# Three-pass fp32r gate and up products in the shared experts of a two-layer perceiver kernel

## The chip, the cores and the metric

The kernel runs as one program on one core of a Trainium2 chip. The metric is the device time of that core in microseconds (us), from the start to the end of an execution; lower is better.

## The reference, cut to what matters

The program computes two layers, each a cross attention, a self attention and a feed-forward step on 512 rows of 512 features. The change touches the feed-forward step of the first layer, a mixture of experts: a router picks 8 of 64 experts for each row, and a shared expert, twice as wide, sees all rows. In short:

```python
scores = sigmoid(x @ gate_w.T)                      # x: 512 rows of the layer norm, E = 64
choice = scores + gate_bias
gmask  = the 4 of 8 groups with the largest sum of their two best choices
topk   = the 8 best of choice * gmask               # weights: scores, normed, times 2.5
routed = sum over e of rw[:, e] * (silu(x @ Wg[e].T) * (x @ Wu[e].T)) @ Wd[e].T   # I = 352
shared = (silu(x @ Sg.T) * (x @ Su.T)) @ Sd.T                                     # 704 wide
x = x + routed + shared
```

All inputs and outputs are fp32.

## The kernel before, in words

Each engine has its own instruction list, written out by hand, and waits on semaphores. Rows are held in four tiles of 128 (`NT = 4`), features in four chunks of 128 (`NC = 4`). `xnT` holds the normed rows turned, features on partitions.

The shared expert is split into two halves of width 352, and with four row tiles that makes eight pieces, k = 0 to 7, with tile t = k // 2 and half hf = k % 2. For each piece TensorE makes a gate group and an up group (`shared_in(k, 0)` and `shared_in(k, 1)`, matmuls at line 755), ScalarE takes the Silu of the gate (`shared_silu`, line 923), VectorE multiplies it with the up product (`shared_mul`, line 1044), TensorE turns the result (`shared_turned`, line 765), ScalarE copies it (`shared_ht`, lines 842 and 843), TensorE multiplies it with the down weights (`shared_out`, line 774) and VectorE adds it to `x` (`shared_add`, line 1048). Matmuls of plain fp32 data are issued twice each, so that a group over four chunks is eight matmuls in the profile.

The pieces are woven by hand into the routing. The routing runs on VectorE as one chain, lines 1055 to 1164, each operation waiting for the one before: scores, group choice, the best 8, the selection table `sel` (line 1091), the weights, then the ranks within the experts that TensorE counts with matrices of ones (lines 800 and 803), the slots, `eot` (line 1119: which expert each tile of rows belongs to), and four steps of one-hot operands (lines 1148 to 1154) from which TensorE makes the index and weight table (`table`, line 781). `shared_mul(0)` stands in this chain ahead of line 1071, `shared_mul(1)` ahead of line 1082, `shared_mul(2)` behind line 1091, `shared_mul(3)` and (4) around line 1122, `shared_mul(5)` behind the second of the four steps, (6) and (7) behind the tables. On TensorE pieces 0 to 5 stand ahead of or between the tables, 6 and 7 behind them.

GpSimd's list ends, in this stage, with the powers of the layer norm (line 337); then come two subtractions for the weights of the next layer (`rest`, line 1261, called with `wkv`), whose rounded halves ScalarE makes at line 932, and then the gathers of rows for the experts (line 2167).

SyncE's list: it writes the normed rows and a block of zeros to DRAM (lines 546 and 547, semaphore `rows_out`), then clears the accumulators (lines 548 and 550), then, when the tile table is known, starts the expert weights. `load_gu(0, 0)`, `load_dn(0, 0)` and `load_gu(0, 1)` wait for nothing more; `load_dn(0, 1)` (line 2118) waits for the last up group of the shared expert (`sh_u` = 8), since its buffer lies in `xnT`; what follows is queued behind it.

The expert loop already works in three passes of fp32r: an operand is rounded to fp32r by ScalarE ("high", `weights_high`, line 2078, `rows_high`, line 2300, `down_high`, line 2335), the rest is made by VectorE ("low", `weights_low`, line 2086, `rows_low`, line 2387), and TensorE adds high x high, high x low and low x high (line 2233). An fp32r matmul is issued once; a group over four chunks is twelve matmuls. At line 2078 the weights of the first expert are rounded into the buffer `wgu_hi[0]`, between `shared_ht(5)` and `shared_silu(6)`.

Of the kernel before, what the change touches and what calls it, by code (L numbers as in the profile page):

```python
# [26 lines left out]
P = 128  # L27
# [26 lines left out]
def perceiver(nc, a, out):  # L54
# [3 lines left out]
    with ExitStack() as ctx:  # L58
# [3 lines left out]
        def sem(name):  # L62
            return ctx.enter_context(nc.semaphore(name))
# [171 lines left out]
        wdn_hi = [m.view(2, D) for _ in range(2)]  # L235
        hT_lo = m.view(2, P)

        wkv_hi, wkv_lo = ([square(S_r, slot_at(i), NC) for i in ii] for ii in ((0, 2), (1, 3)))
# [41 lines left out]
        wbd_ready = sem("wbd_ready"); zpad_set = sem("zpad_set"); rix_ready = sem("rix_ready"); dve_x = sem("dve_x")  # L280
        dve_seq3 = sem("dve_seq3"); dve_seq4 = sem("dve_seq4"); pool_seq4 = sem("pool_seq4")
        ff_x = sem("ff_x"); ff_y = sem("ff_y")
        lg_made = sem("lg_made"); lg_exp = sem("lg_exp"); sel_ready = sem("sel_ready"); rank_made = sem("rank_made")
        ab_ready = sem("ab_ready"); tab_made = sem("tab_made"); eot_ready = sem("eot_ready")
        eot_made = sem("eot_made"); tables = sem("tables"); n_ready = sem("n_ready"); rows_out = sem("rows_out"); acc_out = sem("acc_out")
        sh_g = sem("sh_g"); sh_u = sem("sh_u"); sh_silu = sem("sh_silu"); sh_h = sem("sh_h")
        sh_t = sem("sh_t"); sh_ht = sem("sh_ht"); sh_d = sem("sh_d"); sh_y = sem("sh_y")
# [221 lines left out]


        def first_sync(sp):
            for c in range(NC):
# [39 lines left out]
        def first_pool(pool):  # L552
# [49 lines left out]
            for t in range(NT):  # L602
                ln_pow(pool, 2, t)

        def first_pe(pe):
# [144 lines left out]
            def shared_in(k, gu):  # L750
                t, hf = k // 2, k % 2
                if k >= 2:
                    pe.wait_ge(sh_h if gu else sh_silu, k - 1)
                for c in range(NC):
                    last = nc.tensor.matmul(PS[:, 2 + 2 * hf + gu, 0:I], xnT[:, c, t * P:(t + 1) * P],  # L755
                                            wgu[2 + hf][:, c, gu, :], start=(c == 0), stop=(c == NC - 1))
                last.then_inc(sh_u if gu else sh_g, 1)
# [87 lines left out]
        def first_act(act):  # L845
# [24 lines left out]
            def z_c(L, t):  # L870
                zt_copy(act, NT * L + t, t)

            rows_c(0, 0)
            rows_c(0, 1)
# [35 lines left out]
            z_c(1, 2)  # L910
            probs_c(1, 3)
            z_c(1, 3)
            for t in range(NT):
# [4 lines left out]
            def shared_silu(k):  # L918
# [4 lines left out]
                nc.scalar.activation(sgate[hf], PS[:, 2 + 2 * hf, 0:I], ACT.Silu).then_inc(sh_silu, 1)  # L923

            shared_silu(0)
            for k in range(1, 6):
                shared_silu(k)
                shared_ht(act, k - 1)
                if k == 2:
                    act.wait_ge(ld_wkv, 32)  # L930
                    for i in range(2):
                        nc.scalar.copy(wkv_hi[i], slot[1 + 2 * i][:, :, :]).then_inc(w_hi, 1)
            shared_ht(act, 5)
            weights_high(0, 0)
            shared_silu(6)
            shared_silu(7)
# [3 lines left out]
        def first_dve(dve):  # L940
# [222 lines left out]
            dve.wait_ge(tables, 1)  # L1163
            nc.vector.tensor_copy(cols[:, :, 1], idx_tab[:, 0:NBUF]).then_inc(cols_set, NBUF)  # L1164
            weights_low(0, 0)
            shared_mul(6)
            shared_mul(7)
# [921 lines left out]
        with nc.Block() as block:  # L2089
# [203 lines left out]
            def _(act):  # L2293
# [35 lines left out]
                def down_high(r, k):  # L2329

                    i = NBUF * r + k
                    act.wait_ge(w_dn[k], 32 * (r + 1))
                    if not (isinstance(r, int) and r == 0 and k < 2):
                        act.wait_ge(y_made, i - 1)
                    nc.scalar.copy(wdn_hi[k % 2], wdn[k][:, 0:2, :]).then_inc(dh_ready, 1)
# [175 lines left out]
```

## Time and profile before

| what | value |
|---|---|
| median of 3 runs | 1648.01 us (1646.71 to 1651.56) |
| the profiled execution | 1653.6 us, its span 1651.8 us |
| granted TensorE clock, mean | 0.993 of full speed |
| TensorE busy (matmul) | 1599.3 us, 97% |
| VectorE busy | 1096.3 us, 66% |
| ScalarE busy | 821.3 us, 50% |
| GpSimd busy | 465.2 us, 28% |
| HBM read and written | 207.81 MB and 21.76 MB |

The profile is of one execution, taken by the hardware profiler. Engines are PE (TensorE matmuls), PEld (TensorE weight loads, which overlap PE), DVE (VectorE), ACT (ScalarE), POOL (GpSimd) and SP (SyncE; SPq is its queue of transfers). Times in rows are microseconds from the start of the span unless a column says otherwise. L755 is line 755 of the kernel; S, R and PS are the large SBUF arenas and the PSUM tensor. Busy shares are means over the whole span: the stage of the change lies between about 117 and 210 us, and what a change in it is worth is read from that stage. Matmul ends are modelled, and the spans of GpSimd are rough.

### The profile page before, as it was taken

The numbers are of one execution on the slowest core, as the hardware profiler recorded it, in microseconds if no ns is written. First come the engines' busy times: TensorE is split into PE (matmuls) and PEld (weight loads), VectorE is DVE, ScalarE is ACT, GpSimd is POOL, SyncE is SP. The second block draws the span as 40 slices with busy tenths as digits, with TensorE's granted clock in tenths as the row PEclk, the third lists the DMA queues.
The fourth block names the chain that finished last, engine by engine and source line by source line (L and its number), as shares of the span: only waits on it lengthen the run. The fifth ranks groups of instructions, "written<-read, shape, count | busy, mean of one in ns | idle before, by whom it ended". The sixth has DMA issues, their size and how long they took to land.

```text
span 1651.8 us, 35385 instructions
## 1 busy us (share of the span) xinstructions
PE 1599.3 (97%) x13652; PEld 1406.2 (85%) x13653; DVE 1096.3 (66%) x2217; ACT 821.3 (50%) x1248; POOL 465.2 (28%) x421
## 2 busy tenths in 40 slices
PE   8999999999999999899999999999999999999897
PEld 5666688888888888769999999999999999999583
DVE  3878787787787788655656556565565655656666
ACT  1242177777777777324545445454354544634122
POOL 3012134444544544231413214132041320410100
PEclk9999999999999999999999999999999999999999
DMA  8003399999999999400202002020020100201200
GB/s 308 7 2 122 105 369 337 336 341 343 344 328 339 330 335 314 128 6 3 79 7 81 6 2 81 7 81 7 1 81 7 61 26 2 81 2 42 94 27 26
DMA packets 68858, 214.63 MB, mean 130 GB/s; under 512 B 13618, under 2 KB 31282, under 8 KB 58880
## 3 DMA queue, kind: packets, MB, share of 16 engines
q1 hardware_dynamic: 54400, 196.03, 34.1%
q0 software_dynamic: 14336, 16.83, 4.5%
q8 instruction: 93, 1.52, 0.4%
q14 instruction: 29, 0.24, 0.0%
HBM read 207.81 MB, written 21.76 MB: 139 GB/s over the span
## 4 chain that ended last, share of the span: by engine, by line
PE 81%; DMA 9%; DVE 5%; issue 2%; ACT 1%; SPq 1%; POOL 0%; ACTq 0%; DVEq 0%; POOLq 0%
PE PS L1352 17%; PE PS L1343 17%; PE PS L2233 10%; PE PS L1387 6%; PE PS L1368 6%; PE PS L2259 4%; PE PS L1410 3%; PE PS L400 3%; PE PS L2255 3%; PE PS L458 2%; DMA qbd<-in_w_gu 2%; DMA S<-in_w_gu 2%; DMA R<-in_w_gu 2%; PE PS L421 1%; PE PS L755 1%
## 5 line engine op out<-in xcount | busy, mean ns | idle before, releaser
L1352 PE MATMUL PS<-S_r 128*128 128x256 f32 x2496 | 319.4, 282 | 0.0
L1352 PEld LDWEIGHTS PS<-S_r 128*128 128x128 f32 x2496 | 309.7, 188 | 3.4 <-issue 0.5
L1343 PE MATMUL PS<-S_r 128*128 128x384 f32 (+1 forms) x1536 | 306.5, 349 | 0.0
L1539 DVE SCALAR_TENSOR_TENSOR kq<-PS,bias_c,kq 64x384 fp32r<-64x384 f32 (+1 forms) x256 | 162.3, 634 | 206.7 <-ACT kq L1470 201.9
L1343 PEld LDWEIGHTS PS<-S_r 128*128 128x128 f32 x1536 | 268.3, 188 | 6.5 <-issue 0.5
L2233 PE MATMUL PS<-S_r,R_r 128*128 128x352 f32 x1152 | 273.5, 328 | 0.2 <-DVE R_r L2387 0.2
L1470 ACT ACTIVATE kq<-PS,bias_c 64x384 fp32r<-64x384 f32 (+1 forms) x256 | 151.1, 590 | 197.1 <-PE PS L1343 193.7
L2233 PEld LDWEIGHTS PS<-S_r,R_r 128*128 128x128 f32 x1152 | 198.6, 188 | 3.8 <-DVE R_r L2387 0.5
L2180 POOL DMA_INDIRECT moe_acc<-x,cols x64 | 125.0, 1953 | 220.2 <-ACT x L2318 130.3
L1280 POOL COPY S<-qbd 64x128 f32<-64x128 f32 x128 | 38.3, 299 | 486.0 <-PE PS L1368 467.2
L1261 POOL TENSOR_TENSOR S_r<-S,S_r 128x1536 fp32r<-128x1536 f32 (+2 forms) x31 | 116.9, 3781 | 130.9 <-ACT S_r L1461 107.7
L1549 DVE CUSTOM_DVE_ANT_0 R<-PS,maskadd 128x384 f32<-128x384 f32 (+1 forms) x256 | 136.9, 572 | 3.6 <-PE PS L1368 0.4
L1490 ACT COPY S<-PS 128x512 f32<-128x512 f32 (+1 forms) x128 | 64.6, 505 | 129.0 <-PE PS L1387 127.2
L1484 ACT ACTIVATE R<-R,nmx 128x1601 f32<-128x1601 f32 x64 | 104.0, 1628 | 38.2 <-DVE nmx L1557 37.8
L1368 PE MATMUL PS<-kq 128*128 128x384 f32 (+1 forms) x512 | 120.3, 355 | 2.1 <-POOL kq L1285 1.3
L2086 DVE TENSOR_TENSOR R_r<-R,S_r 128x1408 fp32r<-128x1408 f32 x64 | 101.1, 1622 | 31.7 <-ACT S_r L2078 31.6
L1387 PE MATMUL PS<-ident,R 128*128 128x128 f32 (+1 forms) x832 | 114.9, 275 | 0.0
L2167 POOL DMA_INDIRECT S<-moe_rows,cols x64 | 95.7, 1495 | 68.3 <-DVE cols L1164 32.6
L2078 ACT CAST S_r<-R 128x1408 fp32r<-128x1408 f32 x64 | 84.5, 1368 | 45.9 <-DMA R<-in_w_gu 42.0
L1530 DVE COPY R<-PS 128x256 f32<-128x256 f32 (+1 forms) x124 | 52.5, 424 | 75.6 <-PE PS L1352 75.2
L1584 DVE COPY S<-PS 128x512 f32<-128x512 f32 (+1 forms) x128 | 75.2, 588 | 41.2 <-PE PS L1387 38.8
L1387 PEld LDWEIGHTS PS<-ident,R 128*128 128x128 f32 (+1 forms) x832 | 94.3, 140 | 7.3 <-DVE S L1584 2.2
(250 smaller groups left out, 2610.6 us busy)
## 6 DMA issues: line engine op xcount, KB each, us to landing
R<-in_w_gu SPq DMA_DIRECT2D x34, 1408.0 KB, 16.7
R<-in_w_dna SPq DMA_DIRECT2D x50, 512.0 KB, 17.2
qbd<-in_w_gu SPq DMA_DIRECT2D x16, 1408.0 KB
S<-in_w_gu SPq DMA_DIRECT2D x16, 1408.0 KB
S<-in_ctxT SPq DMA_DIRECT2D x24, 768.0 KB, 4.7
R<-in_w_dnb SPq DMA_DIRECT2D x50, 192.0 KB, 18.7
xnT<-in_w_dna SPq DMA_DIRECT2D x16, 512.0 KB
S<-in_ctxT SPq DMA_DIRECT2D x8, 898.0 KB
```

What stands on the lines that cost most here:

```text
L1261: nc.gpsimd.tensor_tensor(lo, raw, hi.bitcast(F32), ALU.subtract).then_inc(s, 1)
L1343: last = nc.tensor.matmul(PS[:, bank, 0:n], w3[0][:, cc, f0:f0 + P], x3[i][:, cc, 0:n], start=(cc == 0 and w3 is wkv_hi and x3 is ctx_hi), ...
L1352: last = nc.tensor.matmul(PS[:, bank, 0:256], x3[need][:, cc, k0:k0 + P], w3[1][:, cc, f0:f0 + 256], start=(cc == 0 and w3 is wkv_hi and x ...
L1368: last = nc.tensor.matmul(PS[:, p, 0:n], qb[(dc + 1) % 2][half][:, p, :], keys[c % 2][p][:, 0:n], start=(half == 0), stop=(half == 1))
L1387: last = nc.tensor.transpose(PS[0:n, 2 + p, i * P:(i + 1) * P], sx[2 * (dc % 2) + p][:, kt * P:kt * P + n], ident[:, :])
L1470: nc.scalar.activation(keys[c % 2][p][r, 0:n], PS[r, bank_of(b, dc, ("k", c)), 0:n], ACT.Identity, bias=bias_c[r, 3, f:f + 1]).then_inc(kh ...
L1484: nc.scalar.activation(v, v, ACT.Exp, scale=SC, bias=nmx[:, p:p + 1], accum_out=rsx[:, p:p + 1]).then_inc(px_ready, 1)
L1539: nc.vector.scalar_tensor_tensor(out=k[other, 0:n], in0=PS[r, bank_of(b, dc, ("k", c)), 0:n], scalar=bias_c[r, 3, f:f + 1], in1=k[r, 0:n]. ...
L1549: nc.vector.tensor_tensor_reduce(out=sx[2 * ((dc + 1) % 2) + p][:, k0:k0 + n], in0=PS[:, p, 0:n], in1=maskadd[:, k0:k0 + n], scale=1.0, sc ...
L2086: nc.vector.tensor_tensor(wgu_lo[k][:, c, :, :], wgu[k][:, c, :, :], wgu_hi[k % 2][:, c, :, :].bitcast(F32), ALU.subtract).then_inc(wl_rea ...
L2180: pool.indirect_dma_start(out=acc[k % 2], out_offset=bass.IndirectOffsetOnAxis(ap=cols[:, k, 0:1], axis=0), in_=yrow[k], in_offset=None, b ...
L2233: last = nc.tensor.matmul(PS[:, gu, 0:I], x3[:, c, :], w3[:, c, gu, :], start=(c == 0 and x3 is hi[0] and w3 is hi[1]), stop=(c == NC - 1 ...
```

## The change

Gate and up of pieces k = 2 to 7 are made from rounded and rest operands in three fp32r passes, as in the expert loop. Pieces 0 and 1 stay as they were.

- ScalarE rounds the weights of half 1 in one copy ahead of the last attention copy (`shared_high(1)`), and, behind a wait for the row writes (`rows_out` 32), the rows of tile 1 and the weights of half 0 ahead of `shared_silu(0)`, the rows of tiles 2 and 3 behind it. Rounded rows of tile 1 go where the normed rows lay, those of tiles 2 and 3 and the weights of half 1 into idle parts of `qbd` and `kq`, the weights of half 0 into `wgu_hi[0]`.
- GpSimd makes the rests in place, in the order of `SH_LO`: three of rows (512 elements a partition), four of weights (1408 elements), ahead of its two subtractions for `wkv`.
- TensorE waits for `sh_lo` before each of the twelve groups, and issues twelve matmuls in place of eight.
- Since `wgu_hi[0]` is in use until the up group of piece 6, `weights_high(0, 0)` moves behind `shared_silu(6)` and a wait for `sh_u` = 7, and `weights_low(0, 0)` behind `shared_mul(6)`. The first `down_high`, which writes into `kq`, waits for `sh_u` = 8.

```diff
@@ -234,6 +234,10 @@
         m = Arena(kq[:, :])
         wdn_hi = [m.view(2, D) for _ in range(2)]
         hT_lo = m.view(2, P)
+        sgu_hi = [wgu_hi[0], Arena(kq[:, :]).view(NC, 2, I)]
+        sgu_lo = wgu_lo[2:4]
+        xs_hi = [None, Arena(S_r, 14200).view(NC, P)] + [Arena(flat4(qbd_r), NC * 2 * I + i * NC * P).view(NC, P)
+                                                          for i in range(2)]
 
         wkv_hi, wkv_lo = ([square(S_r, slot_at(i), NC) for i in ii] for ii in ((0, 2), (1, 3)))
         m = Arena(R0, 13400 - NC * D)
...
@@ -507,6 +511,8 @@
             nc.vector.tensor_tensor(x[:, t, :], x[:, t, :], PS[:, O_B, :], ALU.add).then_inc(x_ready, 1)
             dve.wait_ge(x_ready, k + 1)
 
+
+        SH_LO = [("x", 1), (0, 0), (0, 1), ("x", 2), (1, 0), (1, 1), ("x", 3)]
 
         def first_sync(sp):
             for c in range(NC):
@@ -601,6 +607,24 @@
                 out_bias(pool, 1, t)
             for t in range(NT):
                 ln_pow(pool, 2, t)
+
+            def shared_rows_low(t):
+                pool.wait_ge(sh_hi, (2, 4, 5)[t - 1])
+                nc.gpsimd.tensor_tensor(xnT_r[:, :, tile(t)], xnT[:, :, tile(t)], xs_hi[t].bitcast(F32),
+                                        ALU.subtract).then_inc(sh_lo, 1)
+
+            def shared_low(hf, gu):
+                pool.wait_ge(sh_hi, 1 if hf else 3)
+                pool.wait_ge(sh_u if gu else sh_g, hf + 1)
+                nc.gpsimd.tensor_tensor(sgu_lo[hf][:, :, gu, :], wgu[2 + hf][:, :, gu, :],
+                                        sgu_hi[hf][:, :, gu, :].bitcast(F32), ALU.subtract).then_inc(sh_lo, 1)
+
+            pool.wait_ge(lg_made, 1)
+            for piece in SH_LO:
+                if piece[0] == "x":
+                    shared_rows_low(piece[1])
+                else:
+                    shared_low(*piece)
 
         def first_pe(pe):
 
@@ -751,9 +775,18 @@
                 t, hf = k // 2, k % 2
                 if k >= 2:
                     pe.wait_ge(sh_h if gu else sh_silu, k - 1)
-                for c in range(NC):
-                    last = nc.tensor.matmul(PS[:, 2 + 2 * hf + gu, 0:I], xnT[:, c, t * P:(t + 1) * P],
-                                            wgu[2 + hf][:, c, gu, :], start=(c == 0), stop=(c == NC - 1))
+                if k < 2:
+                    for c in range(NC):
+                        last = nc.tensor.matmul(PS[:, 2 + 2 * hf + gu, 0:I], xnT[:, c, t * P:(t + 1) * P],
+                                                wgu[2 + hf][:, c, gu, :], start=(c == 0), stop=(c == NC - 1))
+                else:
+                    pe.wait_ge(sh_lo, max(SH_LO.index(("x", t)), SH_LO.index((hf, gu))) + 1)
+                    lo = xnT_r[:, :, t * P:(t + 1) * P]
+                    for c in range(NC):
+                        for x3, w3 in ((xs_hi[t], sgu_hi[hf]), (lo, sgu_hi[hf]), (xs_hi[t], sgu_lo[hf])):
+                            last = nc.tensor.matmul(PS[:, 2 + 2 * hf + gu, 0:I], x3[:, c, :], w3[:, c, gu, :],
+                                                    start=(c == 0 and x3 is not lo and w3 is sgu_hi[hf]),
+                                                    stop=(c == NC - 1 and w3 is sgu_lo[hf]))
                 last.then_inc(sh_u if gu else sh_g, 1)
 
             def shared_turned(k):
@@ -869,6 +902,12 @@
 
             def z_c(L, t):
                 zt_copy(act, NT * L + t, t)
+
+            def shared_high(hf):
+                nc.scalar.copy(sgu_hi[hf], wgu[2 + hf]).then_inc(sh_hi, 1)
+
+            def shared_rows_high(t):
+                nc.scalar.copy(xs_hi[t], xnT[:, :, tile(t)]).then_inc(sh_hi, 1)
 
             rows_c(0, 0)
             rows_c(0, 1)
@@ -909,6 +948,8 @@
             exp_t(1, 3)
             z_c(1, 2)
             probs_c(1, 3)
+            act.wait_ge(ld_sh, 96)
+            shared_high(1)
             z_c(1, 3)
             for t in range(NT):
                 rows_c(2, t)
@@ -922,7 +963,13 @@
                     act.wait_ge(sh_h, k - 1)
                 nc.scalar.activation(sgate[hf], PS[:, 2 + 2 * hf, 0:I], ACT.Silu).then_inc(sh_silu, 1)
 
+            act.wait_ge(rows_out, 32)
+            act.wait_ge(xT_ready, 3 * NT)
+            shared_rows_high(1)
+            shared_high(0)
             shared_silu(0)
+            shared_rows_high(2)
+            shared_rows_high(3)
             for k in range(1, 6):
                 shared_silu(k)
                 shared_ht(act, k - 1)
@@ -931,8 +978,9 @@
                     for i in range(2):
                         nc.scalar.copy(wkv_hi[i], slot[1 + 2 * i][:, :, :]).then_inc(w_hi, 1)
             shared_ht(act, 5)
+            shared_silu(6)
+            act.wait_ge(sh_u, 2 * NT - 1)
             weights_high(0, 0)
-            shared_silu(6)
             shared_silu(7)
             shared_ht(act, 6)
             shared_ht(act, 7)
@@ -1162,8 +1210,8 @@
             nc.vector.tensor_copy(w_tab[:, :], PS[:, 0, TAB + NCOL:TAB + 2 * NCOL]).then_inc(tables, 1)
             dve.wait_ge(tables, 1)
             nc.vector.tensor_copy(cols[:, :, 1], idx_tab[:, 0:NBUF]).then_inc(cols_set, NBUF)
+            shared_mul(6)
             weights_low(0, 0)
-            shared_mul(6)
             shared_mul(7)
             shared_add(2)
 
@@ -2330,6 +2378,8 @@
 
                     i = NBUF * r + k
                     act.wait_ge(w_dn[k], 32 * (r + 1))
+                    if isinstance(r, int) and r == 0 and k == 0:
+                        act.wait_ge(sh_u, 2 * NT)
                     if not (isinstance(r, int) and r == 0 and k < 2):
                         act.wait_ge(y_made, i - 1)
                     nc.scalar.copy(wdn_hi[k % 2], wdn[k][:, 0:2, :]).then_inc(dh_ready, 1)
```

## Rows read from the trace of the kernel before

**Rows 1.** The chain of waits, 110 to 260 us: start, length, engine and line.

```profile
144.43 3.67 DVE S L1091
...
188.52 0.88 DVE S L1154
189.45 2.87 PE PS L781 x16
...
223.09 1.93 PE PS L2233 x12
```

**Rows 2.** TensorE's timeline: start, length, line, operands, count, idle before.

```profile
176.50 2.87 PE L781 MATMUL PS<-S 128*128 128x192 f32 x16 [1.70 <-DVE S L1154]
...
194.73 7.26 PE L755 MATMUL PS<-R,xnT 128*128 128x352 f32 x24
...
202.16 2.53 PE L755 MATMUL PS<-R,xnT 128*128 128x352 f32 x8
204.53 2.74 PE L774 MATMUL PS<-R 128*128 128x512 f32 x6
```

**Rows 3.** Waits of SyncE's queue: total, times, longest.

```profile
SPq L2118 <- PE PS L755: 27.4, 1, 27.4
```

**Rows 4.** SyncE's timeline: start and length of an issue.

```profile
128.05 0.51 SPq L547 DMA_DIRECT2D moe_rows<-S  x1
...
204.86 0.33 SPq L2118 DMA_DIRECT2D xnT<-in_w_dna  x1
```

**Rows 5.** Windows: length, busy PE, PEld, DVE, ACT, POOL; PEclk, DMA share, GB/s.

```profile
130.00:150.00 20.00, 19.59 (x80) 12.72 (x78) 17.38 (x75) 5.81 (x10) 0.00 (x0) 1.00 0.52 183
...
240.00:660.00 420.00, 407.46 (x2271) 355.49 (x2270) 337.52 (x409) 317.63 (x466) 201.01 (x116) 1.00 1.01 335
```

**Rows 6.** ScalarE's timeline.

```profile
120.12 0.58 ACT L476 COPY xnT<-PS 128x512 f32<-128x512 f32 x1 [3.21 <-PE PS L446]
...
130.69 1.28 ACT L923 ACT_TABLE_LOAD   x1
132.71 0.46 ACT L923 ACTIVATE R<-PS 128x352 f32<-128x352 f32 x1 [0.74 <-PE PS L755]
...
189.32 2.64 ACT L2078 CAST S_r<-qbd 128x1408 fp32r<-128x1408 f32 x2
...
213.94 1.06 ACT L2335 CAST kq<-R 128x1024 fp32r<-128x1024 f32 x1
```

**Rows 7.** Line 547, the write of zeros: us from issue to landing.

```profile
DMA to landing us min/median/max: 9.6/9.6/9.6
```

**Rows 8.** VectorE's timeline, routing.

```profile
136.92 0.52 DVE L1044 TENSOR_TENSOR R<-R,PS 128x352 f32<-128x352 f32 x1
...
139.91 0.52 DVE L1044 TENSOR_TENSOR R<-R,PS 128x352 f32<-128x352 f32 x1 [1.27 <-PE PS L755]
...
150.55 6.50 DVE L1101 TENSOR_TENSOR S<-S 128x2048 f32<-128x2048 f32 x1
157.09 2.29 DVE L1102 TENSOR_REDUCE S<-S 128x32 f32<-128x2048 f32 x1
...
159.67 1.83 DVE L1106 TENSOR_SCALAR S<-S 128x64 f32<-128x64 f32 x1
...
165.46 2.28 DVE L1122 TENSOR_TENSOR S<-S 128x2048 f32<-128x2048 f32 x1
```

**Rows 9.** GpSimd's timeline in the routing.

```profile
150.19 11.25 POOL L1261 TENSOR_TENSOR S_r<-S,S_r 128x2048 fp32r<-128x2048 f32 x2 [23.22 <-ACT S_r L932]
```

**Rows 10.** Lines 343 and 1261 on GpSimd: ns shortest/median/longest.

```profile
L343 POOL TENSOR_TENSOR x<-x,bias_r x12: 1264/1271/1647, 21.5 to 1588.5; 128x512 f32<-128x512 f32 x12
...
L1261 POOL TENSOR_TENSOR S_r<-S,S_r x31: 3470/3512/6581, 150.2 to 1434.6; 128x1536 fp32r<-128x1536 f32 x22, 128x1796 fp32r<-128x1796 f32 x7, 128x2048 fp32r<-128x2048 f32 x2
```

**Rows 11.** GpSimd's timeline behind the expert loop.

```profile
668.12 4.01 POOL L1261 TENSOR_TENSOR S_r<-S,S_r 128x1536 fp32r<-128x1536 f32 x1 [2.07 <-ACT S_r L1461]
```

**Rows 12.** VectorE's timeline behind the expert loop.

```profile
671.17 1.03 DVE L1620 TENSOR_TENSOR same_q<-ident 128x64 f32<-128x64 f32 x1
```

More of the change, by code:

```diff
@@ L280, in perceiver @@
         wbd_ready = sem("wbd_ready"); zpad_set = sem("zpad_set"); rix_ready = sem("rix_ready"); dve_x = sem("dve_x")
-        dve_seq3 = sem("dve_seq3"); dve_seq4 = sem("dve_seq4"); pool_seq4 = sem("pool_seq4")
+        dve_seq3 = sem("dve_seq3"); dve_seq4 = sem("dve_seq4");
         ff_x = sem("ff_x"); ff_y = sem("ff_y")
@@ L285, in perceiver @@
         eot_made = sem("eot_made"); tables = sem("tables"); n_ready = sem("n_ready"); rows_out = sem("rows_out"); acc_out = sem("acc_out")
-        sh_g = sem("sh_g"); sh_u = sem("sh_u"); sh_silu = sem("sh_silu"); sh_h = sem("sh_h")
+        sh_hi = sem("sh_hi"); sh_lo = sem("sh_lo"); sh_g = sem("sh_g"); sh_u = sem("sh_u"); sh_silu = sem("sh_silu"); sh_h = sem("sh_h")
         sh_t = sem("sh_t"); sh_ht = sem("sh_ht"); sh_d = sem("sh_d"); sh_y = sem("sh_y")
```

## The prediction

> **What bounds the kernel now.** The change lies between 117 and 210 us of a span of 1651.8 us, so I read the chain of waits of that stretch first. The reader sees there that VectorE's routing, not TensorE, carries most of it: from line 1091 at 144.43 to the last table operand at 188.52 the long pieces are VectorE's, and TensorE takes the chain over only with the last table matmuls at 189.45 [rows 1]. TensorE is nevertheless almost full: a group of eight matmuls of line 755 takes 2.37 us (202.16 to 204.53), it waits 1.70 us for table operands at 176.50, and it goes without a gap from 194.73 to the last up-group at 204.5 [rows 2]. So in this stretch two engines are nearly level, and a gain on TensorE before 189 us is worth nothing unless VectorE also gets faster; only what lies behind the last table counts.
>
> Then the queue of transfers: SyncE waited 27.4 us for the last shared up-group (`sh_u` = 8), and issues the second expert's down weights at 204.86 [rows 3, 4]. From 240 to 660 us the DMA engines are full (share 1.01) while TensorE has 407.5 of 420 us [rows 5]. The expert loop is thus paced by a stream that starts when shared group (7, up) ends, and TensorE's own start in it follows 6 us behind the same event, two output groups (2.7 us each) and two turns. Whatever shifts that event shifts the rest of the kernel one for one. The question is only where it moves.
>
> **TensorE's part.** Groups k = 2 to 7, gate and up, are 12 groups of 2.37 us [rows 2]. Their new form is that of line 2233, 12 matmuls of 128x128 by 128x352, 1.93 us a group [rows 1]. Saved: 12 x 0.44 = 5.3 us. Eight groups stand ahead of the tables, behind VectorE; four (6 and 7) stand behind them: 4 x 0.44 = 1.8 us on the path.
>
> **ScalarE's part.** The high copy of half 1 (2816 elements in one instruction) costs what the two casts of 1408 at line 2078 do, 2.64 us. It is put ahead of the copy at 120.12, which follows 3.21 us of idleness, so it runs from 116.9 to 119.6 [rows 6]. Cost nothing; without that cover at most 2.6 us. The others are not hidden. Behind the exponential, over at 130.7, ScalarE now waits for `rows_out` 32. The zero rows were issued at 128.05 and landed 9.6 us later [rows 4, 7], so it waits until 137.7. Then rows-high of tile 1 (512 elements, about 0.6, between the 0.58 of 512 from PSUM and 1.06 of 1024 within SBUF), the high copy of half 0 (2.6), the table load, which stands directly ahead of the first Silu in the instructions (1.28), and Silu 0.46 [rows 6]: 137.7 + 0.6 + 2.6 + 1.3 + 0.5 = 142.7. Today Silu 0 is over at 133.2 and nobody waits for it. VectorE's shared_mul(0) stands in the middle of the routing, at 136.92, and shared_mul(1) at 139.91 [rows 8]. They move to 142.7 and, with the two further rows-high copies ahead of Silu 1, 144.1: at least 4.2 us later, and the whole routing is queued behind them.
>
> **GpSimd's part, the larger one.** Its subtraction costs 1.27 us for 512 elements, 3.51 for 1536 [rows 10], so 1.27 + 896 x 2.19 ns = 3.2 us for 1408. New are three of 1.3 and four of 3.2: 16.8 us, beside the routing. What such an operation does to VectorE stands in three rows. Line 1101 took 6.50 us while GpSimd ran line 1261's 2048 elements; line 1122, the same shape, 2.28 alone. Line 1106, 64 elements, took 1.83 us and ended when GpSimd did. Line 1620, 64 elements, took 1.03 and ended with GpSimd's 668.12 + 4.01; while line 1102 (a reduction) kept its 2.29 [rows 8, 9, 11, 12]. So VectorE's operation waits for the end of GpSimd's whole one where it reads two SBUF tensors or is a tensor_scalar of an even width; reductions, MAX8, index searches and products with a PSUM operand go through. Between GpSimd's two operations line 1101 got its turn (it ended at 157.05, the second lasted until 161.44), so they alternate.
>
> The Trainium skill says the same in "SBUF — State Buffer", section "Who interferes with whom": the shared port pair is locked for a whole instruction, and a cast or tensor_scalar in a two-port mode takes it too. By that the two casts (lines 1071, 1087) would wait as well; the rows don't show this, and it would make the routing 1.4 us later than below.
>
> By the rows, from there (us): rests of tile 1 138.3 to 139.6, VectorE idle; rest (0, gate) 140.9 to 144.1. Mul 0 ends at 143.1, line 1072 waits to 144.1, ends 144.4. Rest (0, up) to 147.6; line 1076 waits for it, ends 148.05. Tile 2's to 149.3, (1, gate) to 152.5; meanwhile mul 1, MAX8 and the searches, which go through. Line 1089 (2.3) waits for 152.5, ends 154.8. Rest (1, up) to 158.0 lies under the reduction of line 1091, which ends at 158.5, where today it ends at 148.1: +10.4. Tile 3's to 159.3, line 1095 waits for it, ends 159.7. Then the two old rests of wkv (4.6 each by the slope), whose high parts ScalarE casts from 151.5 to 155.2: to 164.3 and, with lines 1097 and 1099 (four elements each) caught once each, to 169.1. Lines 1099 to 1102 end at 174.3 instead of 159.4: +14.9. Today's own stall at line 1106 (1.6 us) is gone by then: eot is ready at 177.8, +13.3, and nothing of GpSimd follows, so the tables end 13.3 later too. TensorE isn't late in this: from 158.5 it has 24 us of matmuls until table 0; even with the group behind eot (177.8) it is through by 187, and table 0's operand comes at 189.8.
>
> Behind the tables: -1.8. weights_high(0, 0), now behind group (6, up), takes 2.64, its rests 3.15 more or less overlapped: done 4.6 us after that group, where TensorE still has 10 us of work (11 today, less two groups' 0.44) ahead of line 2233 (group 7's two, outputs 6 and 7, turns). Hidden; without that cover it would show as a wait at 2233. Its copy delays shared_ht(6) to 4.1 us behind the group, when TensorE wants it at 4.2. The extra waits of down_high and of weights_low find their events past: nothing. SyncE's and GpSimd's gathers wait for the tables, as before.
>
> **Sum.** +13.3 - 1.8 = +11.5 us. The profiled execution took 1653.6 us with a span of 1651.8, so 1665.1 and 1663.3 by its own measure. It was 5.6 us slower than the median of the runs, 1648.0, which gives 1659.5. Bounds of the unknown prices: the routing's shift can't be under the 4.2 us of the Silu less the 5.8 us that today's rests of wkv cost lines 1101 and 1106 (-1.6), nor above 4.2 plus all 16.8 us of new rests (21.0); with the 1.8 behind the tables that is -3.4 to +19.2, or 1644.6 to 1667.2. I take +11.5, since each of its waits is of a kind that the rows show.
>
> **Rivals.**
> 1. GpSimd holds the port between its operations too, since its queue is full: lines 1072 to 1091 start behind its six operations that are in a row from 140.9, at 156.3, sel is ready at 165.6 (+17.5), and with the wkv rests eot is +16.8. Net +15.0: 1663. Against it: line 1101 came between two queued ones [rows 8, 9].
> 2. Only long operations are caught. Then mul 1 at 144.1, line 1089 147.3 to 149.6, sel +5.2, line 1101 held until 157.3, line 1122 until 168.9: +3.4 - 1.8 = +1.7: 1649.7. Against it: 64 elements were caught twice [rows 8, 12].
> 3. The other side: TensorE is the bound. It was idle under 0.5 us from 130 to 150 [rows 5]; if the rests fall beside reductions and `rows_out` lands before the exponential ends, all 12 groups count: -5.3, 1642.7. It decides once VectorE's shift is under the 0.4 to 1.7 us that TensorE waits for it today. Against it: a landing 7 us after the exponential [rows 7], and the chain, which is VectorE's [rows 1].
> 4. The three passes aren't faster here (their weights switch each time, as in line 2233, which speaks against it): +13.3, 1661.3.
>
> **How the numbers follow.** Chances: forecast 0.71, rival 1 0.12, rival 2 0.08, rival 3 0.04, rival 4 0.05. Range 1652.5 to 1665: it leaves out rivals 2 and 3 and takes in the casts (+1.4), rival 1, and a routing caught half as often (+5). One can tell a change of 0.3%, 4.9 us, from none. Slower by more: 0.71 + 0.12 + 0.05 and a quarter of rival 2, 0.90; the rest of rival 2 is "same", 0.06; faster 0.04.
>
> **What would show it.** ScalarE's first rows-high copy starts near 137.7; mul 0 near 142.7; lines 1072, 1076, 1089 and 1097 stretched, each ending with a subtraction of GpSimd; `sel` near 158.5; TensorE idle some 8 us ahead of line 800; SyncE's issue near 216 instead of 204.86. Wrong would be: GpSimd's rests beside lines 1072 to 1089 without a stretched one, `sel` before 153, or a longer expert loop.

## The result, and the profile after

The changed kernel took 1660.78 us (median of 4 runs, 1660.2 to 1662.88), the kernel before 1648.81 in the same comparison: slower by 12.0 us. The ratio estimated from these runs, here and below, is not quite that of the medians (1.0073): it is 1.0065 with a 95% interval of 1.0048 to 1.0082, which is 10.7 us (7.9 to 13.5). The forecast was 1659.5 us, slower by 11.5. The profiled execution took 1661.3 us with a span of 1659.4. It ran the stage ahead of the change 1.42 us sooner than the execution profiled before, so I count places in this stage from the end of the logits (128.83 us after, 130.25 before).

ScalarE's timeline shows the wait for the row writes, the two roundings and the table load ahead of the first Silu; the Silu itself begins at 141.26, where it began at 132.71 before [rows 6].

```profile
136.89 0.62 ACT L910 CAST S_r<-xnT 128x512 fp32r<-128x512 f32 x1 [7.63 <-DMA moe_rows<-S]
137.42 2.53 ACT L907 CAST S_r<-R 128x2816 fp32r<-128x2816 f32 x1
139.97 1.28 ACT L964 ACT_TABLE_LOAD   x1
141.26 0.46 ACT L964 ACTIVATE R<-PS 128x352 f32<-128x352 f32 x1
```

GpSimd's timeline shows the seven new subtractions and, at 157.32, the two old ones:

```profile
137.65 1.28 POOL L613 TENSOR_TENSOR xnT_r<-xnT,S_r 128x512 fp32r<-128x512 f32 x1 [12.10 <-ACT S_r L910]
140.03 6.30 POOL L619 TENSOR_TENSOR R_r<-R,S_r 128x1408 fp32r<-128x1408 f32 x2 [1.10 <-ACT S_r L907]
146.29 1.32 POOL L613 TENSOR_TENSOR xnT_r<-xnT,qbd_r 128x512 fp32r<-128x512 f32 x1
147.57 6.50 POOL L619 TENSOR_TENSOR R_r<-R,kq 128x1408 fp32r<-128x1408 f32 x2
154.04 3.31 POOL L613 TENSOR_TENSOR xnT_r<-xnT,qbd_r 128x512 fp32r<-128x512 f32 x1
157.32 9.18 POOL L1309 TENSOR_TENSOR S_r<-S,S_r 128x2048 fp32r<-128x2048 f32 x2
```

VectorE's timeline of the routing, to be held against [rows 8]. Line 1092 is the product that was line 1044, 1139 was 1091, 1149 was 1101, 1154 was 1106.

```profile
141.81 0.52 DVE L1092 TENSOR_TENSOR R<-R,PS 128x352 f32<-128x352 f32 x1 [6.34 <-issue]
142.25 0.98 DVE L1119 CAST S<-S 128x32 f32<-128x32 uint32 x1
143.27 3.21 DVE L1120 TENSOR_TENSOR S<-S 128x128 f32<-128x128 f32 x1
...
146.83 1.06 DVE L1124 TENSOR_TENSOR S<-S 128x256 f32<-128x256 f32 x1
...
149.91 1.07 DVE L1135 CAST S<-S 128x32 f32<-128x32 uint32 x1
151.01 5.21 DVE L1137 TENSOR_TENSOR S<-S 128x2048 f32<-128x2048 f32 x1
156.26 3.66 DVE L1139 TENSOR_REDUCE S<-S 128x256 f32<-128x2048 f32 x1
...
160.39 1.73 DVE L1143 TENSOR_TENSOR S<-S 128x256 f32<-128x256 f32 x1
...
162.60 3.92 DVE L1145 TENSOR_SCALAR S<-S 128x4 f32<-128x4 f32 x1
...
167.43 2.29 DVE L1149 TENSOR_TENSOR S<-S 128x2048 f32<-128x2048 f32 x1
...
172.34 0.20 DVE L1154 TENSOR_SCALAR S<-S 128x64 f32<-128x64 f32 x1
```

The reader is to see that six operations of 4 to 256 elements (lines 1119, 1120, 1124, 1135, 1143 and 1145) last until a subtraction of GpSimd ends, or up to 0.3 us longer. A seventh, line 1137, gets in when one ends at 154.07 and then does its own 2.2 us, and it holds GpSimd in turn: the 512 elements at 154.04 take 3.31 us instead of 1.3. Line 1120, 0.29 us in the kernel before, takes 3.21, line 1145 with four elements 3.92 and ends at 166.52, as the second old subtraction does at 166.50. The long line 1149 is down to 2.29, since nothing of GpSimd is left by then.

TensorE's timeline has two holes, one ahead of the first turn and one ahead of the ranks, and in the windows (columns as in [rows 5]) its granted clock falls behind them:

```profile
142.39 0.90 PE L798 MATMUL PS<-ident,R 128*128 128x128 f32 x3 [4.03 <-DVE R L1092]
...
159.97 4.53 PE L833 MATMUL PS<-S 128*128 128x64 f32 x20 [7.70 <-DVE S L1139]
```

```profile
130.00:150.00 20.00, 15.93 (x51) 10.63 (x50) 13.28 (x66) 7.19 (x10) 11.25 (x5) 0.83 0.46 167
150.00:170.00 20.00, 12.30 (x53) 10.03 (x52) 19.66 (x12) 4.13 (x4) 16.49 (x5) 0.66 0.00 1
170.00:190.00 20.00, 19.73 (x105) 16.42 (x105) 19.06 (x36) 2.46 (x7) 0.00 (x0) 1.00 0.21 78
```

0.83 and 0.66 are stretches mixed of the two levels, 2.4 and 1.2 GHz, where the kernel before had 1.00 [rows 5]. A three-pass matmul follows the one before at 0.29 us in the first new group, behind the first hole, and at 0.16 in the later ones.

SyncE's issue of the second expert's down weights, and the chain of waits for the four groups behind the tables:

```profile
214.11 0.33 SPq L2166 DMA_DIRECT2D xnT<-in_w_dna  x1
```

```profile
205.93 5.76 PE PS L787 x36
212.02 1.92 PE PS L787 x12
```

214.11 less 128.83 is 85.3 us, against 204.86 less 130.25, 74.6 [rows 4]: the event that starts the stream of expert weights is 10.7 us later. All kernels in this table, worked out from their timelines (us behind the end of the logits; "first product" is the start of `shared_mul(0)`, "issue" that of the second expert's down weights; the clock is that of 150 to 170 us; the medians belong to three comparisons, so compare the ratios):

| kernel | first product | sel | eot | last table ends | issue | clock | median us, ratio |
|---|---|---|---|---|---|---|---|
| before | 6.7 | 17.8 | 34.2 | 62.1 | 74.6 | 1.00 | 1648.0 to 1650.3 |
| the change | 13.0 | 31.1 | 46.7 | 74.5 | 85.3 | 0.66 | 1660.78, 1.0065 |
| e1 no wait | 7.8 | 24.6 | 39.0 | 66.8 | 77.6 | 0.70 | 1653.76, 1.0022 |
| e2 short rests | 13.1 | 23.2 | 39.9 | 67.8 | 78.5 | 0.98 | 1654.68, 1.0028 |
| e3 neither | 6.7 | 18.0 | 36.7 | 64.5 | 75.3 | 0.85 | 1651.17, 1.0011 |
| e4 plain products | 13.5 | 31.6 | 47.1 | 75.6 | 88.1 | 0.76 | 1662.12, 1.0067 |
| e5 rests cut | 13.0 | 25.8 | 44.6 | 72.4 | 83.2 | 0.74 | 1657.55, 1.0051 |
| e9 all cut, no wait | 7.4 | 19.8 | 37.1 | 65.0 | 75.8 | 0.78 | 1651.71, 1.0010 |
| e8 no wait, old late | 7.8 | 24.5 | 35.0 | 66.7 | 77.5 | 0.66 | 1659.34, 1.0049 |
| e11 e8, old cut | 7.8 | 24.5 | 35.1 | 66.7 | 77.4 | 0.67 | 1658.89, 1.0057 |
| e10 e11, filler | 7.8 | 24.6 | 35.1 | 65.8 | 76.6 | 0.83 | 1655.44, 1.0017 |
| b1 old late | 6.7 | 17.9 | 28.4 | 57.7 | 70.2 | 1.00 | 1647.56, 0.9989 |
| b2 b1, three-pass tail | 6.7 | 17.9 | 28.4 | 57.7 | 68.4 | 1.00 | 1646.05, 0.9970 |
| b3 b2, old cut | 6.7 | 17.9 | 28.4 | 57.7 | 68.5 | 1.00 | 1644.66, 0.9968 |

### The profile page after: what moved, and what is told of

It reads as the page before. It is cut to its first block, busy times and chain, and to the rows that moved or that the text cites. A ratio compares the mean times of both kernels' runs of the same rounds, so it can differ in the third digit from the quotient of the medians.

```text
span 1659.4 us, 35513 instructions
## 1 busy us (share of the span) xinstructions
PE 1597.3 (96%) x13700; PEld 1416.5 (85%) x13701; DVE 1102.8 (66%) x2217; ACT 828.2 (50%) x1253; POOL 481.7 (29%) x428
## 4 chain that ended last, share of the span: by engine, by line
PE 79%; DMA 10%; DVE 6%; issue 2%; ACT 1%; SPq 1%; POOL 0%; DVEq 0%; ACTq 0%; POOLq 0%
PE PS L1400 17%; PE PS L1391 17%; PE PS L2281 10%; PE PS L1435 6%; PE PS L1416 6%; DMA R<-in_w_gu 4%; PE PS L2307 4%; PE PS L1458 3%; PE PS L404 3%; PE PS L2303 2%; PE PS L462 2%; DMA qbd<-in_w_gu 2%; PE PS L425 1%; PE PS L2265 1%; DMA S<-in_w_gu 1%
## 5 line engine op out<-in xcount | busy, mean ns | idle before, releaser
L2134 DVE TENSOR_TENSOR R_r<-R,S_r 128x1408 fp32r<-128x1408 f32 x64 | 101.1, 1621 | 34.3 <-ACT S_r L2126 34.2
L1578 DVE COPY R<-PS 128x256 f32<-128x256 f32 (+1 forms) x124 | 52.5, 424 | 75.7 <-PE PS L1400 75.3
```

Source lines behind the costliest of these rows:

```text
L2134: nc.vector.tensor_tensor(wgu_lo[k][:, c, :, :], wgu[k][:, c, :, :], wgu_hi[k % 2][:, c, :, :].bitcast(F32), ALU.subtract).then_inc(wl_rea ...
```

## The experiments

The kernel before, run again beside each group of experiments, took 1650.29 us (e1 to e4), 1649.9 (e5, e8, b1, b2) and 1650.25 (e9, e10, e11, b3).

Theory: the wait in front of the first Silu and GpSimd's subtractions both stretch VectorE's routing, and the three passes give back 1.8 us. First the two causes apart and together taken away.

**e1.** Tile 1's rounded rows in an idle buffer, so no wait:

```diff
-        xs_hi = [None, Arena(S_r, 14200).view(NC, P)] + ...
+        xs_hi = [None, Arena(S_r, WGU1_AT).view(NC, P)] + ...
-            act.wait_ge(rows_out, 32)
```

> The changed kernel with the rounded rows of tile 1 in an idle buffer of their own (the place of the second expert's weights), so that ScalarE need not wait for the row writes before it rounds. Everything else, the seven rests on GpSimd included, as in the change. Counted from the end of the logits. Theory (the wait of ScalarE and the rests of GpSimd both delay VectorE's routing): the first product of the routing chain starts no later than in the kernel before (6.7 us behind the logits instead of 13.0), the rests start 7 us earlier and now stretch other operations of VectorE; sel ends about 26 us behind the logits instead of 31.1, and the time falls by some 5 us to about 1656. Rival (only the rests count, the wait is hidden behind them): sel and the time stay within 1.5 us of the change, 1659 to 1661. Rival (only the wait counts): 1650 or less.

Measured: 1653.76 us, ratio 1.0022 (1.0012 to 1.0033); 2.2 us under the forecast; the first product at 7.8 (6.7 forecast), sel at 24.6, 1.4 sooner than the theory said, issue at 77.6. Both rivals fall. Two of the seven rests now ran beside VectorE's reciprocal and MAX8 (130 to 136 us), which they didn't hold up (1.75 and 2.3 us, as before), but the later ones still stretch it; VectorE's timeline:

```profile
140.72 2.96 DVE L1123 TENSOR_TENSOR S<-S 128x256 f32<-128x256 f32 x1
...
155.28 3.92 DVE L1144 TENSOR_SCALAR S<-S 128x4 f32<-128x4 f32 x1
```

**e2.** The seven rests cut to two elements (TensorE's part of the edit, the rounded operands in all three passes, is left out here):

```diff
-                nc.gpsimd.tensor_tensor(sgu_lo[hf][:, :, gu, :], wgu[2 + hf][:, :, gu, :],
-                                        sgu_hi[hf][:, :, gu, :].bitcast(F32), ALU.subtract)...
+                nc.gpsimd.tensor_tensor(sgu_lo[hf][:, 0, gu, 0:2], wgu[2 + hf][:, 0, gu, 0:2],
+                                        sgu_hi[hf][:, 0, gu, 0:2].bitcast(F32), ALU.subtract)...
```

> The changed kernel with the seven subtractions of GpSimd cut to two elements a partition; TensorE's second and third pass use the rounded operands again, so that the rests are left out of the result and no instruction of TensorE is missing. ScalarE's wait for the row writes stays. Theory: no stretched operation of VectorE ahead of sel; sel ends about 22.5 us behind the logits (31.1 in the change, 17.8 before), the two old rests stall the chain by their 5 to 6 us as before; time +2.8 us over the kernel before, about 1651.5. Rival (the lock is not the cause, ScalarE's wait or the slower TensorE clock is): 1658 or more.

Measured: 1654.68, ratio 1.0028 (1.0015 to 1.004), sel at 23.2, no operation stretched by more than 0.05 us ahead of it. The rival falls: ScalarE's wait is in place, and sel comes 7.9 us sooner than in the change. The time is 3.2 us over the forecast, of which 1.5 are the kernel before itself (1650.3 here, 1648.8 where the forecast began); against it the run is 4.4 us slower, not 2.8. The issue is 3.9 us later than before, because sel was 0.7 late and the old rests cost more than before (6.0 us instead of 5.8).

**e3.** Both edits.

> Both: rounded rows of tile 1 in a buffer of their own, no wait for the row writes, and the seven rests cut to two elements (left out of the result, TensorE's instructions kept). Theory: VectorE's routing runs as in the kernel before, and what remains is the shorter group of TensorE behind the tables, 4 x 0.44 us: 1.8 us faster than before, about 1647; SyncE's issue of the second expert's down weights 73 us behind the logits (74.6 before, 85.3 in the change). TensorE's granted clock stays full in this stretch. Rival (TensorE is the bound there): 5.3 us faster, 1643.5. Rival (the twelve-matmul groups gain nothing here): no faster than before.

Measured: 1651.17, ratio 1.0011 (0.9999 to 1.0023): no gain, which by its time is what the last rival said. But sel is back at 18.0, and from the last table to the issue there are 10.8 us instead of 12.5: the 1.8 us of the four groups are there. What eats them is eot, 2.4 us late, so that the issue is at 75.3 instead of 73. The clock, which I expected full, fell to 0.85. This miss taught the most. VectorE's timeline:

```profile
149.25 4.27 DVE L1144 TENSOR_SCALAR S<-S 128x4 f32<-128x4 f32 x1
...
153.76 4.24 DVE L1146 TENSOR_SCALAR S<-S 128x4 f32<-128x4 f32 x1
```

Two tensor_scalars of four elements were each caught by one of the two old subtractions and cost 8.2 us, where the kernel before lost 5.8 with lines 1101 and 1106. The price is not in VectorE's work but in what GpSimd happens to hold; ScalarE's roundings of these weights, and with them the subtractions, came 0.9 us sooner behind the logits here and shifted the catch.

**e4.** Everything kept but the three passes:

```diff
-                        for x3, w3 in ((xs_hi[t], sgu_hi[hf]), (lo, sgu_hi[hf]), (xs_hi[t], sgu_lo[hf])):
-                            last = nc.tensor.matmul(..., x3[:, c, :], w3[:, c, gu, :], ...)
+                        last = nc.tensor.matmul(..., lo[:, c, :].bitcast(F32), sgu_lo[hf][:, c, gu, :].bitcast(F32), ...)
```

> The changed kernel with all of ScalarE's roundings, GpSimd's rests and every wait, but TensorE multiplies pieces 2 to 7 in plain fp32 as before (on the rests alone, so the rounded part is left out of the result): what the three passes by themselves give. Theory: only the four groups behind the tables count, so 1.8 us slower than the change, about 1662.5, plus at most 0.5 where TensorE's slack ahead of the first table runs out. Rival (all twelve count): 5.3 us slower, 1666. Rival (none counts): the same as the change.

Measured: 1662.12, ratio 1.0067 (1.0047 to 1.0087). The times can't tell it from the change; the traces can: issue 2.8 us later, 1.1 of it ahead of the last table, since table 0 began at 61.8 instead of 58.7 and part of that slack was gone, and 1.8 behind it. So four groups count in full, eight almost not.

**e5.** Each weight rest in four instructions:

```diff
+                for c in range(NC):
+                    last = nc.gpsimd.tensor_tensor(sgu_lo[hf][:, c, gu, :], wgu[2 + hf][:, c, gu, :],
+                                                   sgu_hi[hf][:, c, gu, :].bitcast(F32), ALU.subtract)
```

> The changed kernel with each of the four weight rests on GpSimd cut into four instructions of 352 elements, nothing else. Theory (VectorE waits for the end of the one instruction of GpSimd that runs): no operation of VectorE ahead of sel is stretched by more than 0.9 us at a catch, 3.0 us at most in the change; the sum of the stretches falls from 9 to about 4, though GpSimd's own time rises by 1 to 2 us; sel 27.5 us behind the logits instead of 31.1; 3.5 us faster than the change, 1658. Rival (the two share the port by halves, whatever the length of an instruction): sel and time as in the change.

Measured: 1657.55, ratio 1.0051 (1.0031 to 1.0071), sel at 25.8 instead of 31.1. The intervals of this ratio and the change's overlap, so it is sel and the lines that decide: the stretches ahead of sel sum to 2.7 us instead of 8.2 (about 4 forecast; the longest is 1.0, line 1139), and the sharing rival falls. Behind sel the two old rests, uncut, cost more here, and the issue is only 2.1 us sooner. VectorE's 256-element product of line 1126, which took 1.06 us in the change, and line 1139, 5.21 there:

```profile
145.33 0.72 DVE L1126 TENSOR_TENSOR S<-S 128x256 f32<-128x256 f32 x1
...
148.72 3.30 DVE L1139 TENSOR_TENSOR S<-S 128x2048 f32<-128x2048 f32 x1
```

**b1.** The kernel before, its two old rests behind the first gathers:

```diff
-                for i in range(2):
-                    rest(wkv_lo[i], slot[1 + 2 * i], wkv_hi[i], w_lo, w_hi, i + 1)
                 n = iterations(pool)
                 for k in range(NBUF):
                     gather(0, k)
+                for i in range(2):
+                    rest(wkv_lo[i], slot[1 + 2 * i], wkv_hi[i], w_lo, w_hi, i + 1)
```

> The kernel before with nothing changed but the place of GpSimd's two old subtractions (the next layer's weights, 2048 elements each): behind the first four gathers, in a stretch in which VectorE mostly waits, instead of beside the routing. Theory (a whole-instruction hold of the port by GpSimd is what stretches VectorE's operations): line 1101 falls from 6.50 to 2.3 us and line 1106 from 1.83 to 0.2, eot is ready 28.5 us behind the logits instead of 34.2. TensorE then becomes the later one (its fp32 groups, and the one-hot buffers that wait for tables), so that only about 2.9 of these 5.8 us reach the last table: 1647.4 where the kernel before takes 1650.3. Rival (line 1101 is slow for another reason, such as its operands): no change in lines 1101 and 1106, no change in time.

Measured: 1647.56 against 1649.9, ratio 0.9989 (0.9979 to 0.9998). The two lines fell as forecast, eot came at 28.4, and 4.4 of the 5.8 us reached the issue, more than the 2.9 that I gave TensorE; by the medians 2.3 us of them reached the time. VectorE's timeline:

```profile
150.12 2.29 DVE L1101 TENSOR_TENSOR S<-S 128x2048 f32<-128x2048 f32 x1
...
155.02 0.20 DVE L1106 TENSOR_SCALAR S<-S 128x64 f32<-128x64 f32 x1
```

**b2.** b1, and three passes for pieces 6 and 7 alone, rests by VectorE (the edit in part):

```diff
+            if k == 5:                        # ScalarE, behind Silu 5
+                nc.scalar.copy(xs3_hi, xnT[:, :, tile(3)]).then_inc(sh_hi, 1)
+                for hf in range(2):
+                    nc.scalar.copy(sgu_hi[hf], wgu[2 + hf]).then_inc(sh_hi, 1)
...
+            shared_low(0, 0)                  # VectorE, behind its last one-hot operand
             dve.wait_ge(tab_made, NT)
...
+            shared_low(0, 1); shared_low(1, 0); shared_low(1, 1)
             shared_mul(6)
             weights_low(0, 0)
```

> As b1_old_rests_late, and three passes for pieces 6 and 7 alone, the four groups behind the tables. ScalarE rounds both halves' weights and the rows of tile 3 in its idle time behind Silu 5, VectorE makes the rests behind its last one-hot operand, where it waits; GpSimd does nothing for them. Theory: 1.8 us under b1, SyncE's issue of the second expert's down weights some 4.7 us earlier than in the kernel before (69.9 behind the logits), the time 0.3% under the kernel before: 1645.5. Rival (VectorE's five rests, 7.1 us, are on the path behind the tables): no faster than b1.

Measured: 1646.05 against 1649.9, ratio 0.9970 (0.9958 to 0.9982); the issue is 1.8 us ahead of b1's, and 6.2 ahead of the kernel before, of which 3.9 reach the time. The times of b1 and b2 alone don't separate them (the intervals just overlap). TensorE waits 2.35 us for a rest in the first expert. **b3** is b2 with the old rests in eight instructions of 512 elements.

> As b2_tail_only, with the two old subtractions cut into eight of 512 elements. In b2 they held the rests of the second expert's weights (5.34 us instead of 3.15) and TensorE waited 2.35 us in the first expert. Theory: that wait falls under 1 us, 1.5 us under b2: 1644.5, 0.33% under the kernel before. Rival (the gain is lost again in the loop, whose transfers set the pace): as b2.

Measured: 1644.66 against 1650.25, ratio 0.9968 (0.9954 to 0.9982). The wait is 1.77, only 0.6 us better and not under 1 as forecast, so whether b3 beats b2 stays open; both beat both kernels. TensorE's timeline of b2 and of b3:

```profile
211.95 3.27 PE L2263 MATMUL PS<-S_r,R_r 128*128 128x352 f32 x11 [2.35 <-DVE R_r L2419]
```

```profile
211.10 3.27 PE L2267 MATMUL PS<-S_r,R_r 128*128 128x352 f32 x12 [1.77 <-DVE R_r L2423]
```

**e8.** e1 with the old rests late, as in b1.

> The changed kernel without the wait for the row writes (as e1) and with the two old subtractions of GpSimd behind the first gathers (as b1). Theory: against e1, lines 1142 to 1149 lose the 3.9 us that they were stretched there, sel stays 24.6 us behind the logits, eot comes at 35 instead of 39.0 and the issue at 73.9 instead of 77.6: a little faster than the kernel before (74.6), 1649.5. Rival (the new rests go on stretching the routing behind sel): as e1.

Measured: 1659.34, ratio 1.0049 (1.003 to 1.0068), 10 us over the forecast, and the largest miss. eot came at 35.0 as expected, but the issue at 77.5, as in e1, and by the medians the run is 5.6 us slower than e1. Two reasons are in VectorE's timeline:

```profile
168.80 0.52 DVE L1091 TENSOR_TENSOR R<-R,PS 128x352 f32<-128x352 f32 x1 [3.77 <-PE PS L787]
...
204.57 11.24 DVE L2133 TENSOR_TENSOR qbd_r<-qbd,S_r 128x1408 fp32r<-128x1408 f32 x2 [0.82 <-ACT S_r L2125]
```

At 168.80 VectorE waits for piece 3's up product (line 787): TensorE, idle for 8 us ahead of the ranks, works on at a clock of 0.66 (its first 20 matmuls of the ranks take 4.53 us, 2.44 in the kernel before) and has become the later one. That is the issue. What lies behind it is the second: at 204.57 the rests of the first expert's weights, which the change has moved to this place, meet the moved old ones and take 11.24 us instead of 3.15, and TensorE begins the first expert's products 14.6 us behind the issue, where it is 5.6 in the kernel before, in the change and in e1.

**e11.** e8 with the old rests in eight instructions.

> As e8, with the two old subtractions of GpSimd, behind the first gathers, cut into eight of 512 elements. In e8 they held VectorE's rests of the first expert's weights for 11.2 us instead of 3.2, since the change has moved those to the same place. Theory (the end of the one instruction is waited for): that pair takes about 5.5 us, TensorE starts the expert loop some 5.5 us earlier than in e8, time about 1653.5. What stays of e8's miss is TensorE: granted clock 0.66 between 150 and 170 us after its 8 us of idleness ahead of the ranks, the ranks and pieces 3 at half speed, and VectorE waiting 3.8 us for piece 3's up product; the issue stays 77.5 us behind the logits. Rival (the pair was slow for the copies of ScalarE): time as in e8, 1659.

Measured: 1658.89, ratio 1.0057 (1.0042 to 1.0073). My theory of the cure failed. GpSimd's timeline and VectorE's:

```profile
203.57 9.88 POOL L2239 TENSOR_TENSOR S_r<-S,S_r 128x512 fp32r<-128x512 f32 x8
```

```profile
204.40 12.07 DVE L2133 TENSOR_TENSOR qbd_r<-qbd,S_r 128x1408 fp32r<-128x1408 f32 x2 [0.82 <-ACT S_r L2125]
```

Here VectorE did not get its turn between the eight instructions, though in e5 and b3 it did; it waited until the last had ended at 213.45. ScalarE's roundings of these weights were over at 205.64, so they are not the reason, though the rival named the right time. e10, with the same eight instructions, repeats it (10.55 us for the first of the pair), and in e8 it waited through both whole ones. Why it is let in at one place and not at the other no run here tells.

**e10.** e11 with eight matmuls of TensorE into an idle bank ahead of the ranks:

```diff
+            for i in range(8):
+                nc.tensor.matmul(PS[:, 1, :], ident[:, :], zero512, start=True, stop=True)
             pe.wait_ge(sel_ready, 1)
```

> As e11, and TensorE has eight more matmuls of 128 by 512 in fp32, about 7 us, into an unused bank, where it otherwise idles for the selection table. Theory (the fallen clock makes TensorE the bound of this kernel): granted clock near 1.0 from 150 to 170, ranks in 2.4 us instead of 4.5, no wait of VectorE for piece 3, issue at 74 us behind the logits instead of 77.5, time 3.5 us under e11. Rival (the clock is paid by nobody, since TensorE waits anyway): the same time as e11.

Measured: 1655.44 (1647.56 to 1660.67), ratio 1.0017 (1.0004 to 1.0031). The median lies 3.5 us under e11's as forecast, but the trace doesn't bear that out: the issue is only 0.85 us earlier, and TensorE begins the first expert 0.4 us earlier. The runs of e10 scatter over 13 us and the profiled one is the slowest of the twelve, so where the 3.5 us come from stays open, and the theory isn't shown. The filler held the clock for most of the ranks' first part (2.74 us), and it fell behind them all the same, so six matmuls of 512 columns took 5.08 us instead of 2.8:

```profile
154.64 2.74 PE L835 MATMUL PS<-S 128*128 128x64 f32 x20 [1.17 <-DVE S L1140]
...
158.88 5.08 PE L807 MATMUL PS<-R 128*128 128x512 f32 x6
```

**e9.** e1 with all rests cut, in their place.

> The changed kernel without the wait for the row writes, all of GpSimd's weight rests in pieces of 352 elements and the two old ones in pieces of 512, in their place beside the routing. Theory: what is left of the routing's stretch is about 4 us ahead of sel and 2 to 3 behind it; sel 21 us and eot 35 us behind the logits, issue 73.5; with the 1.8 us of TensorE level with the kernel before or 1 us under it: 1649.5. Rival (many short instructions catch VectorE as long in sum as few long ones): as e1, 1653.8.

Measured: 1651.71, ratio 1.0010 (1.0001 to 1.0018). sel at 19.8 was 1.2 better than expected, eot at 37.1 two later; the change, so mended, is still not faster than before. The old rests cost most of it; VectorE's timeline has three operations of 64 elements, 0.74 us elsewhere:

```profile
160.63 3.73 DVE L1157 SCALAR_TENSOR_TENSOR S<-S 128x64 f32<-128x64 f32 x3
```

## Why the prediction was right

- **What bounds.** Right. The last table moved by 12.5 us, the issue by 10.7 (11.5 forecast), the time by 10.7 by the ratio and 12.0 by the medians. That the issue shifts the rest one for one held here and within about 1 us in e1 to e3, but not everywhere: of 4.4 us gained at the issue b1 kept 2.3, of 6.2 b2 kept 3.9, and e8 lost 6.5 more behind it. TensorE's saving ahead of the tables is worth nothing (e4: 1.1 of 3.5 us, and only since the slack was eaten).
- **The four groups behind the tables.** Right: 5.76 us for three and 1.92 for the fourth, 1.93 forecast; 12.45 less 10.67 is 1.8.
- **ScalarE.** Right. Copy at 8.1 us behind the logits (7.4 forecast), first product at 13.0 (12.4). The early rounding of half 1 was hidden.
- **GpSimd.** The mechanism was right, by e1, e2 and e5; its sizes were off in both directions, and that they made up for each other was luck. sel moved by 13.2 us, not 10.4: the stretches ahead of it sum to 8.2 us where my steps have about 6, and the first product was 0.5 later. The Trainium skill's page "SBUF — State Buffer", section "Who interferes with whom", says that a cast in a two-port mode takes the pair too; I had left that out of the sum, and the trace agrees with the page: the casts of lines 1119 and 1135 took 0.98 and 1.07 us (0.18 before). It cost more than the 1.4 us that I gave it, for, as the order of the rows has it, the cast used up the turn between two subtractions that line 1120 had in my steps, and line 1120 was caught by the whole of the next one. Against that, I had the old rests catch VectorE twice for about 8.6 us; they caught it twice, lines 1143 and 1145, for 5.1. So eot moved by 12.5, not 13.3.
- **Why the two causes don't add at the issue.** At sel they nearly do: against e3 the wait alone costs 5.2 us (e2), the rests alone 6.6 (e1), both together 13.1. At the issue it is 3.2, 2.3 and 10.0. Between the two stand the old rests, which by where they happened to catch VectorE cost 8.2 us in e3, 6.0 in e2, 3.8 in e1 and 5.1 in the change. e3 had lost the most by them, so each single cause looks cheap against it.
- **Not foreseen.** The fall of TensorE's clock. In the change it costs nothing: from eot to the end of the last table there are 27.8 us in both kernels. So it is in e1, e5 and e9, at 0.70 to 0.78. In e8 the same stretch takes 31.7, 3.8 us more; how much of that is the clock and how much that TensorE starts the ranks late is not separated, and e10, with a clock of 0.83, still takes 30.7. In b1, at full clock, TensorE is the later one too, with 29.3.
- **Rivals.** The back-to-back rival puts sel at 35.3 us behind the logits and eot at 51; 31.1 and 46.7 were measured, and the forecast, 28.2 and 47.5, is nearer in both. But sel lies between the two, and e11 shows that VectorE can be passed over. Rival 2 is out, four elements were caught. Rival 3 is out by e3, rival 4 by e4.

## What to carry to other kernels

A subtraction on GpSimd beside a chain of small VectorE operations cost up to nearly its own length per operation, however small that was (four elements: 4.1 us of a 4.5 us subtraction in e3), and in e8 and e11 an operation waited through more than one: put it beside reductions, MAX8 or PSUM operands, or in a place where VectorE waits, and look again whenever another instruction is moved. Before shortening an engine's work, find the event behind which it is last, and shorten only what stands behind that. An edit that only reorders (b1) gained 0.1%, small but beyond its interval, where the whole change lost 0.65%; three passes for the last two pieces alone (b2, b3) gained 0.3%.

## What the runs showed of the hardware

- GpSimd held VectorE's 1408-element subtraction through eight instructions in a row (e11, 10.53 us for one of the pair, and e10), yet let VectorE in between instructions in e5 and b3. In b3 the two took turns, and each was held by the other (VectorE's 1408 elements 2.72 us instead of 1.6, GpSimd's 512 elements 2.65 instead of 1.26).
- The granted clock fell to 0.66 over 150 to 170 us behind 7.7 us without a matmul, and also to 0.85 in e3, where TensorE was busy for 19.3 of the 20 us and had been idle for 1.40 just ahead of them, before the ranks (0.41 in the kernel before); in b1, busy with fp32 groups for all 20, it stayed at 1.00. Keeping the engine busy ahead of the ranks (e10) gave 0.83, not 1.00.
